# Products of the identity with itself in six waits of TensorE in the first stage of a quantised cross-attention and expert kernel

## The chip, the cores and the metric

The kernel runs on one core of one Trainium2 chip. The metric is the device time of one execution in microseconds (us). A core has TensorE (PE, matrix products; PEld is its weight load), VectorE (DVE), ScalarE (ACT), GpSimd (POOL) and SyncE (SP, which here only issues DMAs). Each engine works through its own instruction stream in order; semaphores tie the streams together. TensorE writes into eight banks of PSUM (`bank0` to `bank7`, `A[0]` to `A[7]` in the code), from which DVE and ACT read. [...]

## The reference, cut to what matters

Four batches of 256 tokens with 256 features go through two residual blocks. The first, per batch, is a gated pair of int8-style linear layers ("smooth quant"): each operand is scaled by factors of its columns' largest magnitudes, rounded row by row to -127..127, multiplied, and scaled back. The second is a mixture of eight experts with low-rank additions to shared base weights, two experts per token.

```
def _smooth_quant_linear(x, w):
    amax_x = max(abs(x), axis=0);  amax_w = max(abs(w), axis=0)
    s = sqrt(maximum(amax_x, EPS) / maximum(amax_w, EPS))
    xs = x / s;  ws = w * s
    x_scale = max(abs(xs), axis=-1) / 127;  w_scale = max(abs(ws), axis=-1) / 127
    return round(xs / x_scale) @ round(ws / w_scale).T * x_scale * w_scale.T

gate, up = split(_smooth_quant_linear(xe, guw));  a = silu(gate) * up
x = x + tanh(g_xattn) * _smooth_quant_linear(a, dw)      # per batch, on layernorm(x)
x = x + tanh(g_ffn) * experts(layernorm(x))              # g = x@base_gate + x@gate_A[e]@gate_B[e]*0.25, ...
```

## The kernel before

All streams are written out by hand, one function per engine; what an engine does next is the next line of its function, and it waits there for the semaphores named.

The first stage (to about 55 us) is the first block, batch by batch (`b` = 0 to 3, two tiles of 128 tokens each), with the batches interleaved. For TensorE one batch is this sequence:

- `w_T(b)`, `x_T1(b)`, `c_T(b)`: transposes of the weights, of the normalised tokens and of the second weight, from which DVE takes the column maxima (`w_max`, `x_max`, `c_max`; `c_max` increments `s_camax`). `c_T(b)` writes bank `4 + b`.
- `factors(b)` (line 1520): four f32 products that spread the smoothing factors (computed on POOL) over all partitions, each with the identity `ident` as moving operand. DVE's `smooth(b)` (lines 1077 to 1084) multiplies by them, takes row maxima and their inverses.
- `q1_T(b)` (line 1537): eight transposes in two halves of the values that ACT scaled (line 694), into banks `b` and `4 + b`. ACT copies them out as bf16 (line 702).
- `row_w(b)` (1520, two products), `products1(b)` (1550): the row of weight scales, and the quantised product itself. DVE (1092), ACT (709, 719) and DVE (1098, `act_up`) scale it back, apply silu and multiply.
- `a_T(b)` (1557): two transposes of the result, for DVE's `a_max` (1109, 1110). From it POOL makes the second factors (519).
- `factors2(b)` (1520), then DVE `smooth2` (1116 to 1121), ACT (724), `q2_T(b)` (1569), ACT (731), `row_c(b)` (1520), `products2(b)` (1582). DVE then adds the residual and normalises again (`x1_rows`, `x1_norm`, 1128 to 1146).
- `x2_T(b)` (1590) transposes the normalised tokens for the second block; ACT (741) and DVE (1151) split them into two parts.

From about 55 us TensorE runs 32 `unit`s, the products with the shared base weights (lines 56, 58, 60, called as `split_product`), six products of 448 columns each, with the last pieces of the first stage and the routing logits between the first of them. DVE computes the routing from the logits (lines 1224 to 1313), and POOL then gathers the sorted tokens (561). The expert tiles follow to the end.

Bank 7 (`A[7]`) holds `w_T(3)` and `c_T(3)` at first, and is written again by the second half of `q1_T(3)` and by the routing counts at line 1712. Bank 4 is written by `c_T(0)` and then by the second half of `q1_T(0)`.

Of the kernel before, what the change touches and what calls it, by code (L numbers as in the profile page):

```python
# [32 lines left out]
P = 128  # L33
# [16 lines left out]
def products_of(m):  # L50

    def split_product(outs, hi, lo, whi, wlo, first, last):

        n = len(outs)
        for i in range(n):
            m.matmul(outs[i], hi, whi[i], start=first, stop=False, skip_group_check=True)  # L56
        for i in range(n):
            m.matmul(outs[i], hi, wlo[i], start=False, stop=False, skip_group_check=True)  # L58
        for i in range(n):
            ins = m.matmul(outs[i], lo, whi[i], start=False, stop=last, skip_group_check=True)  # L60
        return ins

    return split_product


def build(nc, x, fside, ctxw, g_xattn, g_ffn, wealth, conf_W, conf_b,
          base_gate, base_up, base_down, gate_A, gate_B, up_A, up_B, down_A, down_B, xn, gun, yg, out):
    NB, S, H = x.shape
    I2 = ctxw.shape[2]
    E, _, R = gate_A.shape  # L70
    I = base_gate.shape[1]
    ER = E * R
# [17 lines left out]
    with stack:  # L90
        def sem(name):
            return stack.enter_context(nc.semaphore(name))

        def sb(name, shape, dt=F32, scope=stack):
            return scope.enter_context(nc.sbuf_tensor(name, shape, dt))

        def ps(name, shape, dt=F32, scope=stack):
            return scope.enter_context(nc.psum_tensor(name, shape, dt))
# [3 lines left out]
        ident = sb("ident", [P, P])  # L102
# [26 lines left out]
        with part1:  # L129
            def s1(name, shape, dt=F32):  # L130
                return sb(name, shape, dt, part1)
# [37 lines left out]
            count = s1("count", [P, G])  # L169
# [96 lines left out]
        with psum:  # L266
            A = [ps(f"bank{i}", [P, 512], F32, psum) for i in range(8)]
# [18 lines left out]
        s_wamax, s_xamax, s_camax, s_ratio, s_srs = sem("s_wamax"), sem("s_xamax"), sem("s_camax"), sem("s_ratio"), sem("s_srs")  # L286
# [1196 lines left out]
        def _(pe):  # L1483
            m = nc.tensor
            pe.wait_ge(s_ident, 1)
            pe.wait_ge(s_identb, 1)
            split_product = products_of(m)

            def w_T(b):
                pe.wait_ge(d_w[b], 16)  # L1490
                for c in range(HC):
                    for j in range(TB):
                        ins = m.transpose(A[4 + b][:, c * S + j * P:c * S + (j + 1) * P], q1[:, b, 2 + j, c * P:(c + 1) * P], ident[:, :])
                ins.then_inc(s_wT, 1)

            def x_T1(b):
                pe.wait_ge(s_xn, TB * (b + 1))
                if b == NB - 1:
                    pe.wait_ge(s_cWT, 1)
                for c in range(HC):  # L1500
                    for j in range(TB):
                        ins = m.transpose(A[b][:, c * S + j * P:c * S + (j + 1) * P], q1[:, b, j, c * P:(c + 1) * P], ident[:, :])
                ins.then_inc(s_xT1, 1)

            def c_T(b):
                pe.wait_ge(d_c[b], 16)
                pe.wait_ge(s_wamax, b + 1)
                for j in range(TB):
                    ins = m.transpose(A[4 + b][:, j * P:(j + 1) * P], q2[:, b, 2 + j, :], ident[:, :])
                ins.then_inc(s_cT, 1)  # L1510
# [7 lines left out]
            def along_rows(to, column, unit_rows):  # L1518

                return m.matmul(to, column.to_broadcast([P, P]), unit_rows[:, :], start=True, stop=True)  # L1520

            def factors(b):
                pe.wait_ge(s_srs, b + 1)
                for w in range(2):
                    for c in range(HC):
                        o = (w * HC + c) * P
                        ins = along_rows(A[b][:, o:o + P], s_rs[:, b, c, w:w + 1], ident)
                ins.then_inc(s_bc, 1)

            def q1_T(b):  # L1530
                pe.wait_ge(s_camax, b + 1)
                for w in range(2):
                    pe.wait_ge(s_scaled, 4 * b + 2 * w + 2)
                    for c in range(HC):
                        for j in range(TB):
                            o = (c * TB + j) * P
                            ins = m.transpose(A[b + 4 * w][:, o:o + P], q1[:, b, 2 * w + j, c * P:(c + 1) * P], ident[:, :])
                    ins.then_inc(s_q1Tp, 1)
# [7 lines left out]
            def products1(b):  # L1546
                pe.wait_ge(s_q1T, 2 * b + 2)
                for j in range(TB):
                    for c in range(HC):
                        ins = m.matmul(A[b][:, j * S:(j + 1) * S], q1T[:, b % 2, 0, c, j * P:(j + 1) * P],  # L1550
                                       q1T[:, b % 2, 1, c, :], start=(c == 0), stop=(c == HC - 1))
                ins.then_inc(s_mm1, 1)

            def a_T(b):
                pe.wait_ge(s_a, b + 1)
                for j in range(TB):
                    ins = m.transpose(A[b][:, j * P:(j + 1) * P], q2[:, b, j, :], ident[:, :])
                ins.then_inc(s_aT, 1)
# [7 lines left out]
            def q2_T(b):  # L1566
                pe.wait_ge(s_scaled2, 4 * b + 4)
                for i in range(4):
                    ins = m.transpose(A[4 + b][:, i * P:(i + 1) * P], q2[:, b, i, :], ident[:, :])
                ins.then_inc(s_q2Tp, 1)  # L1570

            def row_c(b):
                pe.wait_ge(s_q2T, b + 1)
                pe.wait_ge(s_identg, 1)
                for j in range(TB):
                    ins = along_rows(A[4 + b][:, j * P:(j + 1) * P], sc2[:, b, 2 + j:3 + j], identg)
                ins.then_inc(s_cbc, 1)

            def products2(b):
                pe.wait_ge(s_q2T, b + 1)  # L1580
                for j in range(TB):
                    ins = m.matmul(A[b][:, j * H:(j + 1) * H], q2T[:, b % 2, 0, j * P:(j + 1) * P], q2T[:, b % 2, 1, :],
                                   start=True, stop=True)
                ins.then_inc(s_mm2, 1)
# [47 lines left out]
            def base(t):  # L1632

                for u in range(4 * t, 4 * t + 4):
                    unit(u)

            w_T(0)
            x_T1(0)
            w_T(1)
# [7 lines left out]
            c_T(1)  # L1647
            c_T(2)
            c_T(3)
            q1_T(0)  # L1650
            factors(1)
            row_w(0)
            products1(0)
            factors(2)
            x_T1(3)
            q1_T(1)
            a_T(0)
            row_w(1)
            products1(1)
# [3 lines left out]
            row_w(2)  # L1663
            products1(2)
            q2_T(0)
            row_c(0)
            products2(0)
            a_T(1)
            q1_T(3)
            factors2(1)  # L1670
# [52 lines left out]
            for g in range(NG):  # L1723
                ins = m.matmul(A[6][:, 0:4 * PT], atrow[:, g, :], attrib[:, g].rearrange("p a j -> p (a j)"),
                               start=(g == 0), stop=(g == NG - 1))
# [6 lines left out]
            for g in range(NG):  # L1732
                ins = m.matmul(A[6][:, 256:256 + 3 * LATE], atrow[:, g, :], lateb[:, g].rearrange("p a i -> p (a i)"),
                               start=(g == 0), stop=(g == NG - 1))
# [186 lines left out]
            for i in range(LATE):  # L1921
                pe.wait_ge(s_ylo, i + 1)
                for b in range(NB):
                    for y in (y_hi, y_lo):
                        for t in range(TB):
                            q = (TB * b + t) * P
                            ins = m.matmul(late_bank(b)[:, t * H:(t + 1) * H], onehot[:, i, q:q + P], y[:, i, :],
                                           start=(i == 0 and t == 0 and y is y_hi), stop=(i == LATE - 1), skip_group_check=True)
# [34 lines left out]
```

## Time and profile before

| | |
|---|---|
| timed runs | 267.85, 271.71, 272.23 us (median 271.71) |
| profiled execution | 270.51 us; span from the first to the last instruction 268.3 us |
| mean granted clock of TensorE over the span | 0.959 |
| PE busy | 239.5 us (89%), 1550 matmul records |
| DVE, ACT, POOL busy | 192.0 (72%), 180.6 (67%), 138.7 us (52%) |
| chain that ended last, by engine | PE 67%, DVE 11%, DMA 7%, POOL 6% |

The span is the time between the first and the last instruction of the program on the core; the time of an execution has about 2.2 us around it. In a timeline each row stands for one or several like instructions in a row: start from the span's beginning, length from the first one's start to the last one's end, engine, source line, operation, what is written and read, and how many. A bracket gives the idle time of the engine just ahead of it and what ended the wait. Matmuls overlap: a row lasts past the start of the next, so the time that a group takes on TensorE is read from start to start.

### The profile page before, as it was taken

The numbers are of one execution on the slowest core, as the hardware profiler recorded it, in microseconds if no ns is written. First come the engines' busy times: TensorE is split into PE (matmuls) and PEld (weight loads), VectorE is DVE, ScalarE is ACT, GpSimd is POOL, SyncE is SP. The second block draws the span as 40 slices with busy tenths as digits, with TensorE's granted clock in tenths as the row PEclk, the third lists the DMA queues.
The fourth block names the chain that finished last, engine by engine and source line by source line (L and its number), as shares of the span: only waits on it lengthen the run. The fifth ranks groups of instructions, "written<-read, shape, count | busy, mean of one in ns | idle before, by whom it ended". The sixth has DMA issues, their size and how long they took to land.

```text
span 268.3 us, 5005 instructions
## 1 busy us (share of the span) xinstructions
PE 239.5 (89%) x1550; PEld 218.2 (81%) x1550; DVE 192.0 (72%) x403; ACT 180.6 (67%) x390; POOL 138.7 (52%) x160
## 2 busy tenths in 40 slices
PE   0748596899989999999998999999999999999883
PEld 0647384699979998889987999999999999998772
DVE  2799968797668962437786687777777777777664
ACT  2738989889674545858998576666666666665450
POOL 4787865684851011278573645884444555531051
PEclk9997868589999999999999999999999999999998
DMA  5963541646897557555527325555555555440644
GB/s 150 331 187 79 124 129 34 170 114 233 248 263 267 205 191 284 174 151 184 176 61 274 104 96 176 176 178 176 178 176 177 177 177 172 159 161 20 187 148 156
DMA packets 31348, 45.78 MB, mean 171 GB/s; under 512 B 14104, under 2 KB 25760, under 8 KB 31328
## 3 DMA queue, kind: packets, MB, share of 16 engines
q0 software_dynamic: 4416, 21.50, 23.9%
q1 hardware_dynamic: 20752, 14.03, 18.7%
q10 hardware_dynamic: 6160, 9.98, 10.4%
q8 instruction: 13, 0.21, 0.4%
q14 instruction: 7, 0.06, 0.1%
HBM read 33.57 MB, written 11.93 MB: 170 GB/s over the span
## 4 chain that ended last, share of the span: by engine, by line
PE 67%; DVE 11%; DMA 7%; POOL 6%; issue 4%; ACT 3%; ACTq 1%; SPq 0%; DVEq 0%; POOLq 0%
PE pY L56 6%; PE pY L58 6%; PE pY L60 6%; PE bank L56 5%; PE bank L58 5%; PE bank L60 5%; PE pT L1800 4%; PE bank L1520 3%; POOL held_B L605 3%; PE pG L1789 2%; PE pG L1790 2%; DMA xin<-normed,tok 2%; PE pU L1790 2%; PE pU L1789 2%; DMA yr<-results 2%
## 5 line engine op out<-in xcount | busy, mean ns | idle before, releaser
L56 PE MATMUL pY<-Wd_hi,hT_hi 128*128 128x320 f32 (+1 forms) x126 | 42.0, 334 | 0.1
L60 PE MATMUL pY<-Wd_hi,hT_lo 128*128 128x320 f32 (+1 forms) x126 | 39.7, 315 | 0.0
L58 PE MATMUL pY<-Wd_lo,hT_hi 128*128 128x320 f32 (+1 forms) x126 | 39.7, 315 | 0.0
L569 POOL DMA_INDIRECT bin<-base_products,tok x18 | 24.8, 1376 | 23.0 <-DVE hbuf L1370 21.6
L561 POOL DMA_INDIRECT xin<-normed,tok x19 | 18.5, 972 | 30.3 <-DVE share L1313 14.0
L575 POOL DMA_INDIRECT results<-yb,dest x17 | 16.9, 992 | 24.6 <-ACT yb L919 23.3
L752 ACT COPY brow<-bank 128x448 f32<-128x448 f32 x32 | 16.9, 531 | 14.2 <-PE bank L60 13.7
L1380 DVE TENSOR_TENSOR hT_lo<-pT,hT_hi 128x512 fp32r<-128x512 f32 (+1 forms) x38 | 23.4, 619 | 3.2 <-ACT hT_hi L896 2.3
L56 PE MATMUL bank<-Wbase_hi,x2T_hi 128*128 128x448 f32 x64 | 24.8, 387 | 0.2 <-ACT brow L752 0.2
L56 PEld LDWEIGHTS pY<-Wd_hi,hT_hi 128*128 128x128 f32 x126 | 23.7, 188 | 0.6 <-ACT Wd_lo L885 0.5
L58 PEld LDWEIGHTS pY<-Wd_lo,hT_hi 128*128 128x128 f32 x126 | 23.8, 189 | 0.0
L60 PEld LDWEIGHTS pY<-Wd_hi,hT_lo 128*128 128x128 f32 x126 | 23.7, 188 | 0.0
L58 PE MATMUL bank<-Wbase_lo,x2T_hi 128*128 128x448 f32 x64 | 23.3, 364 | 0.0
L60 PE MATMUL bank<-Wbase_hi,x2T_lo 128*128 128x448 f32 x64 | 23.2, 363 | 0.0
L1385 DVE TENSOR_TENSOR zT_lo<-pY,zT_hi 128x128 fp32r<-128x128 f32 x18 | 5.2, 291 | 24.4 <-ACT zT_hi L913 24.4
L896 ACT CAST hT_hi<-pT 128x512 fp32r<-128x512 f32 (+1 forms) x38 | 20.8, 549 | 1.4 <-PE pT L1800 1.3
L491 POOL TENSOR_TENSOR WB<-raw,WB 128x448 fp32r<-128x448 f32 x16 | 18.0, 1141 | 7.0 <-ACT WB L663 6.9
L1800 PE MATMUL pT<-ident,hbuf 128*128 128x128 f32 x133 | 20.6, 272 | 0.0
L1375 DVE TENSOR_TENSOR hbuf<-hbuf,gb 128x896 f32<-128x896 f32 x18 | 19.5, 1083 | 0.1
L1365 DVE TENSOR_TENSOR gb<-pG,bin 128x896 f32<-128x896 f32 x18 | 19.4, 1080 | 0.0
L1370 DVE TENSOR_TENSOR hbuf<-pU,bin 128x896 f32<-128x896 f32 x18 | 19.4, 1079 | 0.0
L1800 PEld LDWEIGHTS pT<-ident,hbuf 128*128 128x128 f32 x133 | 16.7, 141 | 3.1 <-DVE hbuf L1444 0.3
(331 smaller groups left out, 723.1 us busy)
## 6 DMA issues: line engine op xcount, KB each, us to landing
base_products<-brow ACTq DMA_DIRECT2D x16, 448.0 KB, 3.6
yr<-results SPq DMA_DIRECT2D x8, 256.0 KB, 5.6
raw<-in_L_ffn_gate_B_dram SPq DMA_DIRECT2D x8, 224.0 KB, 2.5
raw<-in_L_ffn_up_B_dram SPq DMA_DIRECT2D x8, 224.0 KB, 2.7
raw<-in_L_ffn_down_A_dram SPq DMA_DIRECT2D x7, 256.0 KB, 4.6
x_resid<-in_x_dram SPq DMA_DIRECT2D x4, 256.0 KB, 5.1
q<-in_fside_BxS2xS_dram ACTq DMA_DIRECT2D x4, 256.0 KB, 6.8
normed<-q ACTq DMA_DIRECT2D x4, 256.0 KB, 3.9
```

The costliest lines, as they stand in the source:

```text
L56: m.matmul(outs[i], hi, whi[i], start=first, stop=False, skip_group_check=True)
L58: m.matmul(outs[i], hi, wlo[i], start=False, stop=False, skip_group_check=True)
L60: ins = m.matmul(outs[i], lo, whi[i], start=False, stop=last, skip_group_check=True)
L491: g.tensor_tensor(lo, src, hi, ALU.subtract).then_inc(s_wlo, 1)
L561: g.indirect_dma_start(out=xin[:, :], out_offset=None, in_=xn, in_offset=bass.IndirectOffsetOnAxis(ap=tok[:, j:j + 1], axis=0)).then_inc(d ...
L569: g.indirect_dma_start(out=bin_[:, (j + 1) % 2].rearrange("p a i -> p (a i)"), out_offset=None, in_=gun, in_offset=bass.IndirectOffsetOnAx ...
L896: a.copy(hT_hi[:, h_chunks(i), :].rearrange("p c q -> p (c q)"), h_bank(i)).then_inc(s_hhi, 1)
L1365: v.tensor_tensor(halves(gb[:, :]), pG[:, :, 0:IH], halves(bin_[:, 1 - slot, 0, :]), ALU.add).then_inc(s_gadd, 1)
L1370: v.tensor_tensor(halves(hbuf[:, :]), pU[:, :, 0:IH], halves(bin_[:, 1 - slot, 1, :]), ALU.add).then_inc(s_uadd, 1)
L1375: v.tensor_tensor(hbuf[:, :], hbuf[:, :], gb[:, :], ALU.mult).then_inc(s_h, 1)
L1380: v.tensor_tensor(hT_lo[:, h_chunks(i), :].rearrange("p c q -> p (c q)"), h_bank(i), hT_hi[:, h_chunks(i), :].rearrange("p c q -> p (c q)" ...
L1800: ins = m.transpose(pT[:, i, (c % 4) * P:(c % 4 + 1) * P], hbuf[:, c * P:(c + 1) * P], ident[:, :])
```

## The change

In the function of TensorE a helper `spare_products(bank, count)` issues `count` f32 products of the 128x128 identity with itself into the first 128 columns of a bank. Nothing reads the result. It is called six times: 30 products ahead of `q1_T(0)` into bank 4, and into bank 7 seven ahead of `x_T1(3)`, five ahead of `q1_T(1)`, nine ahead of `a_T(0)`, five ahead of `row_c(0)` and eight ahead of `a_T(1)`, 64 in all. Two waits on `s_camax` stand ahead of the first and the second call, so that DVE has read what the bank held. Nothing else changes on any engine.

```
@@ -1486,6 +1486,11 @@
+            def spare_products(bank, count):
+
+                for _ in range(count):
+                    m.matmul(bank[:, 0:P], ident[:, :], ident[:, :], start=True, stop=True, skip_group_check=True)
+
             def w_T(b):
@@ -1647,13 +1652,19 @@
             c_T(1)
             c_T(2)
             c_T(3)
+            pe.wait_ge(s_camax, 1)
+            spare_products(A[4], 30)
             q1_T(0)
             factors(1)
             row_w(0)
             products1(0)
             factors(2)
+            pe.wait_ge(s_camax, NB)
+            spare_products(A[7], 7)
             x_T1(3)
+            spare_products(A[7], 5)
             q1_T(1)
+            spare_products(A[7], 9)
             a_T(0)
             row_w(1)
             products1(1)
@@ -1663,8 +1674,10 @@
             row_w(2)
             products1(2)
             q2_T(0)
+            spare_products(A[7], 5)
             row_c(0)
             products2(0)
+            spare_products(A[7], 8)
             a_T(1)
             q1_T(3)
             factors2(1)
```

The order of TensorE's stream before, from `c_T(3)` (line 1509, bank 7) to `products1(0)`:

```order
L1509 MATMUL bank7<-ident,q2 128x128 x2
L1537 MATMUL bank0<-ident,q1 128x128 x4
L1537 MATMUL bank4<-ident,q1 128x128 x4
L1520 MATMUL bank1<-ident,s_rs 128x128 x4
L1520 MATMUL bank4<-ident,sc1 128x128 x2
L1550 MATMUL bank0<-q1T 128x256 x4
```

The same place after the change, where the lines of the file stand five further down:

```order
L1514 MATMUL bank7<-ident,q2 128x128 x2
L1492 MATMUL bank4<-ident 128x128 x30
L1542 MATMUL bank0<-ident,q1 128x128 x4
L1542 MATMUL bank4<-ident,q1 128x128 x4
L1525 MATMUL bank1<-ident,s_rs 128x128 x4
L1525 MATMUL bank4<-ident,sc1 128x128 x2
L1555 MATMUL bank0<-q1T 128x256 x4
```

The thirty products stand between the last transposes of the second weights and `q1_T(0)`; a row names each operand once, so `bank4<-ident` has the identity as both. TensorE's stream before, from `q2_T(0)` (line 1569) to the first half of `q1_T(3)`:

```order
L1569 MATMUL bank4<-ident,q2 128x128 x4
L1520 MATMUL bank4<-identg,sc2 128x128 x2
L1582 MATMUL bank0<-q2T 128x256 x2
L1557 MATMUL bank1<-ident,q2 128x128 x2
L1537 MATMUL bank3<-ident,q1 128x128 x4
```

And after the change:

```order
L1574 MATMUL bank4<-ident,q2 128x128 x4
L1492 MATMUL bank7<-ident 128x128 x5
L1525 MATMUL bank4<-identg,sc2 128x128 x2
L1587 MATMUL bank0<-q2T 128x256 x2
L1492 MATMUL bank7<-ident 128x128 x8
L1562 MATMUL bank1<-ident,q2 128x128 x2
L1542 MATMUL bank3<-ident,q1 128x128 x4
```

Five products stand ahead of `row_c(0)` and eight between `products2(0)` and `a_T(1)` (line 1562).

## Rows read from the trace of the kernel before

**Rows 1.** Table by stretches: length, busy us of each engine, granted clock, DMA, GB/s.

```profile
21.10:24.52 3.42, 3.42 (x16) 3.21 (x16) 3.21 (x12) 3.42 (x8) 2.73 (x3) 0.50 0.13 29
24.52:31.34 6.82, 4.00 (x30) 3.07 (x28) 6.45 (x15) 5.36 (x12) 5.54 (x9) 1.00 0.52 117
31.34:38.17 6.83, 6.21 (x28) 5.62 (x29) 4.69 (x14) 5.99 (x12) 6.08 (x6) 0.50 0.43 121
38.17:45.00 6.83, 4.45 (x33) 3.13 (x31) 5.52 (x13) 6.17 (x16) 1.85 (x3) 1.00 0.28 84
45.00:55.24 10.24, 8.65 (x35) 7.02 (x36) 8.53 (x23) 9.15 (x19) 7.09 (x8) 0.50 0.42 115
55.24:117.00 61.76, 61.00 (x397) 55.16 (x397) 39.70 (x124) 40.98 (x86) 24.10 (x28) 1.00 0.68 216
...
44.50:50.00 5.50, 3.81 (x15) 2.77 (x15) 5.29 (x15) 4.65 (x11) 5.29 (x7) 0.55 0.31 83
```

**Rows 2.** Timeline of TensorE: start, length, line, instruction, [idle before, what ended it].

```profile
14.50 1.06 PE L1520 MATMUL bank<-ident,s_rs 128*128 128x128 f32 x8
15.39 0.60 PE L1502 MATMUL bank<-ident,q 128*128 128x128 f32 x4
15.83 0.82 PE L1509 MATMUL bank<-ident,q 128*128 128x128 f32 x6
21.10 2.00 PE L1537 MATMUL bank<-ident,q 128*128 128x128 f32 x8 [4.46 <-ACT q L694]
22.91 1.83 PE L1520 MATMUL bank<-ident,s_rs 128*128 128x128 f32 x8
...
27.69 0.66 PE L1502 MATMUL bank<-ident,q 128*128 128x128 f32 x4 [1.11 <-ACT q L677]
29.15 0.63 PE L1537 MATMUL bank<-ident,q 128*128 128x128 f32 x4 [0.81 <-ACT q L694]
...
31.96 0.69 PE L1557 MATMUL bank<-ident,q 128*128 128x128 f32 x2 [1.26 <-DVE q L1098]
32.54 1.23 PE L1520 MATMUL bank<-ident,sc 128*128 128x128 f32 x4
...
39.49 0.66 PE L1569 MATMUL bank<-ident,q 128*128 128x128 f32 x4
40.93 0.71 PE L1520 MATMUL bank<-identg,sc 128*128 128x128 f32 x4 [0.78 <-ACT q2T L731]
...
42.95 0.44 PE L1557 MATMUL bank<-ident,q 128*128 128x128 f32 x2 [1.09 <-DVE q L1098]
...
49.57 1.11 PE L1590 MATMUL bank<-ident,q 128*128 128x128 f32 x4 [0.92 <-DVE q L1146]
```

**Rows 3.** Timeline of DVE in the first stage.

```profile
24.87 1.28 DVE L1077 TENSOR_TENSOR q<-q,bank 128x512 f32<-128x512 f32 x2 [0.20 <-PE bank L1520]
...
34.81 0.88 DVE L1092 SCALAR_TENSOR_TENSOR hq<-bank,sc,rowb 128x256 f32<-128x256 f32 x2 [1.02 <-ACT rowb L709]
...
37.23 0.18 DVE L1121 RECIPROCAL inv<-sc 128x4 f32<-128x4 f32 x1
38.74 1.28 DVE L1077 TENSOR_TENSOR q<-q,bank 128x512 f32<-128x512 f32 x2 [1.33 <-PE bank L1520]
...
42.48 0.41 DVE L1098 TENSOR_TENSOR q<-bank,hq 128x256 f32<-128x256 f32 x1
43.42 0.42 DVE L1109 TENSOR_REDUCE amx<-bank 128x1 f32<-128x256 f32 x1 [0.53 <-PE bank L1557]
```

**Rows 4.** Timeline of ACT in the first stage.

```profile
23.24 1.25 ACT L702 ACTIVATE q1T<-bank,rounder 128x512 bf16<-128x512 f32 x2
```

**Rows 5.** Timeline of POOL: the first gather of rows.

```profile
95.80 1.23 POOL L561 DMA_INDIRECT xin<-normed,tok  x1 [14.03 <-DVE share L1313]
```

**Rows 6.** Timeline of TensorE: the first transposes of gathered rows.

```profile
100.68 0.42 PE L1750 MATMUL pX<-ident,xin 128*128 128x128 f32 x2
```

**Rows 7.** DMA issues: queue, operation, count, median us from issue to landing.

```profile
xin<-normed,tok POOLq DMA_INDIRECT x19, 4.3
```

More of the change, by code:

```diff
@@ L1487, in _, with spare_products @@
             split_product = products_of(m)
+            def spare_products(bank, count):
+                for _ in range(count):
+                    m.matmul(bank[:, 0:P], ident[:, :], ident[:, :], start=True, stop=True, skip_group_check=True)
             def w_T(b):
@@ L1649, in _ @@
             c_T(3)
+            pe.wait_ge(s_camax, 1)
+            spare_products(A[4], 30)
             q1_T(0)
@@ L1654, in _ @@
             factors(2)
+            pe.wait_ge(s_camax, NB)
+            spare_products(A[7], 7)
             x_T1(3)
+            spare_products(A[7], 5)
             q1_T(1)
+            spare_products(A[7], 9)
             a_T(0)
@@ L1665, in _ @@
             q2_T(0)
+            spare_products(A[7], 5)
             row_c(0)
             products2(0)
+            spare_products(A[7], 8)
             a_T(1)
```

## The prediction

> **What bounds the kernel now.** I read the table by stretches first, cut where the granted clock changes [rows 1]. TensorE falls to half clock three times in the first stage: at 21.10, after it had stood idle for 4.46 us [rows 2]; at 31.34, after a stretch in which it worked 4.00 of 6.82 us; and at 45.00, after 4.45 of 6.83 us. It is back at full clock at 24.52, 38.17 and 55.24. [...] From 55.24 to 117.00 it works 61.00 of 61.76 us at full clock. So an earlier or later start of the base products at 55 moves everything behind it, as long as nothing else becomes the limit.
>
> The first stage itself is not TensorE's. The timeline of its instructions [rows 2] has a wait in brackets before each of the six places: 4.46, 1.11, 0.81, 1.26, 0.78 and 1.09 us, all ended by ACT or DVE. The DVE timeline [rows 3] shows the counterpart: DVE waits 0.20, 1.33 and 0.53 us for TensorE, and 1.02 us for ACT. From 44.5 to 50.0 DVE works 5.29 of 5.50 us [rows 1], and TensorE waits 0.92 us for it before 49.57 [rows 2].
>
> **The price of one filler.** No instruction of before multiplies the identity by itself. The nearest row is L1520: f32, 128x128, with the identity as the moving operand. Four of them are issued by `factors(0)`, and the trace records eight matmuls: from 14.50 to the next row at 15.39, 0.89 us, so 0.2225 us for one at full clock [rows 2]. A transpose, also f32 128x128, has one record: four from 15.39 to 15.83, 0.11 us each. A filler is not marked as a transpose, so I take 0.2225; 0.11 is the lower bound. At half clock the eight records of `factors(1)` span 1.83 us instead of 1.06 [rows 2]; less the 0.17 by which the row at 14.50 outlasts the next start, 0.41 us for one, the upper bound.
>
> [...]
>
> **The change, run by run.** The 64 fillers cost 64 x 0.2225 = 14.2 us, and the six waits hold 9.5 us. Each run is therefore longer than its wait. The two new semaphore waits cost nothing: the maximum over the first context block was taken before `c_T(3)` could start, and the last one lies on DVE before the row at 24.87, where TensorE needs it only after 26.
>
> First run: the six transposes at 15.83 end their issue at 16.49. 30 x 0.2225 = 6.68, so `q1_T(0)` starts at 23.17 instead of 21.10, 2.07 late. It and `factors(1)` now run at full clock: 8 x 0.11 = 0.88, then 1.06 as at 14.50, done at 25.11. Before they were done at 22.91 + 1.83 = 24.74 [rows 2]. Behind them waits DVE (row at 24.87, only 0.20 idle before it): about 0.3 late. On ACT the copies at 23.24 [rows 4] now wait for the first half of `q1_T(0)`, 23.17 + 0.44 + 0.17 = 23.78; they take 1.25, so `row_w(0)` starts at about 25.07 and with `row_w(0)` 0.45, `products1(0)` 0.44 and `factors(2)` 0.89 the next run of fillers can start at 26.85.
>
> Second to fourth run: 7 x 0.2225 = 1.56, so `x_T1(3)` starts at 28.41 instead of 27.69. Nobody waits for it: the waits of DVE there [rows 3] are for other work. It takes 0.44, then five fillers 1.11: `q1_T(1)` at 29.96 instead of 29.15, and with 0.88 it is issued by 30.84. Nine fillers, 2.00: `a_T(0)` at 32.84 instead of 31.96, 0.9 late. At full clock it takes 0.22 instead of 0.58, so DVE's maximum over it is 0.6 late. That is covered by the 1.02 us that DVE waits for ACT before 34.81; without that cover the 0.6 would go on.
>
> What comes back: in 31.34 to 38.17 TensorE was at half clock for 6.21 us of work [rows 1]. At full clock it has the factors of block 3 well before DVE wants them, so the 1.33 us that DVE waited before 38.74 are gone. DVE is then bound by itself: its instruction at 37.23 ends at 37.41, plus the 0.3 above, 37.7 instead of 38.74 [rows 3]. Gain on DVE: 1.0 us, so its product at 42.48 is done at 41.9 instead of 42.9.
>
> Fifth and sixth run: `q2_T(0)` follows ACT and DVE and stays where it was, from 39.49; 0.44, then five fillers 1.11, 41.04 against 40.93 for `row_c(0)`; 0.45 and 0.22 for `row_c(0)` and `products2(0)`, 41.71. Now `a_T(1)` could run at 41.95, with DVE's gain. But eight fillers stand before it: 41.71 + 1.78 = 43.49, against 42.95. It is **0.5 late instead of 1.0 early**, and DVE's maximum at 43.42, which waited for it already, is 0.5 late too. This run decides: it takes the whole gain and half a microsecond more.
>
> Behind it no run of fillers stands until the base products. DVE, with next to no idle time between 44.5 and 50 [rows 1], brings `x2_T(0)` at 49.57 0.5 late. TensorE again waits for it, as in 45.00 to 55.24, where it worked 8.65 of 10.24 us at half clock; so I expect the clock to fall between 45 and 50 and to be back at about 55. The base products start 0.5 later, but less of their work lies ahead of the rise: 0.5 us at half clock become 0.25 at full. The end of the stage is then 0.25 to 0.5 late, I take 0.4. With TensorE busy from there to 117.00, and no stage behind with a new instruction, it goes through to the end.
>
> The sum: 270.5 (the profiled execution; its span is 268.3, 2.2 lie around it) + 0.4 = **270.9**. That execution stands 1.2 below the median of the timed runs, 271.71.
>
> **The rivals.** *The clock comes back later.* TensorE's work before 55.24 now begins 0.5 late, and the stretch had 1.6 us without work already [rows 1]. If the rise slips, it is at least by the shortest stretch at half clock in the trace, 3.4 us. Half of that, 1.7, is lost on base products: 270.5 + 0.4 + 1.7 = 272.6. For it: the work that preceded the rise begins later, the rise does not wait for it. Against: the waits behind 49.57 are the same ones. It decides if the clock is still at half at 56.
>
> *A filler has one record, as a transpose has*: 0.11 us. The runs are then 3.3, 0.8, 0.6, 1.0, 0.6 and 0.9 us, each within its wait, and nothing is late. DVE keeps its 1.0 us; `a_T(1)` runs at 40.93 + 0.67 + 0.88 = 42.5, 0.45 early: 270.1. Against: the L1520 rows.
>
> *Full clock through 45 to 55 as well*, since TensorE enters it with less idle behind it. It is then limited by the first gather of rows, issued at 95.80 behind DVE's routing: at the median of 4.3 us to landing its data are there at 100.1, and TensorE takes them at 100.68 [rows 5 to 7]. With DVE 0.5 late they are there at 100.6, so no more than 0.1 is gained: 270.4. Against: none of the waits behind 43 is filled.
>
> *The fillers don't hold the clock*, so that it falls as before and the thirty run mostly at half clock: 30 x 0.41 = 12.3 us, `q1_T(0)` at 28.8, 7.7 late, little of it covered since DVE stands behind it: about 278. It decides if the clock falls before about 20. Against: full clock at 14.50 to 16.5 was reached and held by transposes and L1520 alone.
>
> **How the numbers follow.** The forecast 0.57, the late rise 0.2, the short filler 0.08, full clock throughout 0.05, fillers that don't hold it 0.05, and 0.05 for a gain that I don't see. A measurement of this kernel can tell about 2%, 5.4 us, from no change; its three runs lie from 267.85 to 272.23. Only the fillers at half clock are slower by more, only the unseen gain faster: slower 0.05, faster 0.05, within 2% 0.90. The range: the forecast less what the lowest run lies below the profiled one (270.9 - 2.7 = 268.2), up to the late rise with a little for the upper runs, 273.0.
>
> **What would show it.** In the profile after: 128 records of fillers, 0.11 us apart; `q1_T(0)` at about 23.2; full clock from 14 to past 45; DVE's smoothing of block 3 near 37.7 with no wait for TensorE before it; `a_T(1)` near 43.5, straight behind fillers; a fall of the clock between 45 and 50 and a rise near 55 (near 58 in the first rival). The prediction is wrong if the fillers have 64 records or lie further apart, if DVE's gain at 37.7 is missing, if `a_T(1)` comes before 42.95, or if the clock falls in the first run.

## The result, and the profile of the changed kernel

The changed kernel takes 272.62 us (median of 4 runs, 271.51 to 275.00) against 271.58 us for the kernel before on the same chip (4 runs); ratio 1.0121, 95% interval 1.0066 to 1.0177. Timed once more with 12 runs against 35 it took 272.84 us against 271.37: ratio 1.0079, 1.0042 to 1.0116. The ratios leave out runs classed as slow (8 of those 35, none of the 12), and stand above the ratios of the medians given, 1.0038 and 1.0054. So the changed kernel is slower, by 0.4 to 1.2%. The time lies in the predicted range, and within 2% as forecast, but the sum had said +0.4 us for the change. The loss is 1.0 and 1.5 us by the medians, 1.6 us between the two profiled executions, and 2.1 to 3.3 us by the ratios.

| | before | after |
|---|---|---|
| profiled execution | 270.51 us | 272.15 us |
| span | 268.3 us | 269.9 us |
| mean granted clock over the span | 0.959 | 0.979 |
| PE busy | 239.5 us (89%), 1550 records | 248.2 us (92%), 1678 records |
| at half clock (granted 0.50) ahead of 117 us | 21.10:24.52, 31.34:38.17, 45.00:55.24 | 50.51:57.34, 77.82:81.23 |

The mean clock is higher and the time is longer. The table by stretches of the kernel after (length; busy us of PE, PEld, DVE, ACT, POOL; granted clock; DMA share; GB/s) answers [rows 1]:

```profile
22.90:50.51 27.61, 22.41 (x191) 20.61 (x189) 23.23 (x60) 23.72 (x51) 19.99 (x23) 1.00 0.37 96
46.50:50.51 4.01, 1.18 (x11) 0.74 (x8) 3.87 (x12) 2.06 (x6) 3.84 (x5) 1.00 0.40 114
50.51:57.34 6.83, 6.28 (x24) 5.11 (x24) 5.13 (x14) 5.45 (x11) 3.94 (x6) 0.50 0.51 134
57.34:77.82 20.48, 19.88 (x136) 18.47 (x135) 13.33 (x33) 16.45 (x36) 13.30 (x16) 1.00 0.74 225
77.82:81.23 3.41, 3.41 (x11) 3.05 (x10) 3.02 (x11) 1.66 (x4) 1.17 (x2) 0.50 1.15 263
```

The first two stretches at half clock of before are gone. The third has moved: it no longer lies on the waits of the first stage but from 50.51 to 57.34, over the first base products. A new one, 77.82 to 81.23, lies wholly on base products. TensorE's timeline shows why the third moved; it answers [rows 2] (lines stand five further down, L1492 is the identity product):

```profile
15.22 1.12 PE L1514 MATMUL bank<-ident,q 128*128 128x128 f32 x6
16.18 6.86 PE L1492 MATMUL bank<-ident 128*128 128x128 f32 x60
22.88 1.04 PE L1542 MATMUL bank<-ident,q 128*128 128x128 f32 x8
...
28.27 0.60 PE L1507 MATMUL bank<-ident,q 128*128 128x128 f32 x4
28.71 1.28 PE L1492 MATMUL bank<-ident 128*128 128x128 f32 x10
29.82 1.04 PE L1542 MATMUL bank<-ident,q 128*128 128x128 f32 x8
30.70 2.17 PE L1492 MATMUL bank<-ident 128*128 128x128 f32 x18
32.71 0.38 PE L1562 MATMUL bank<-ident,q 128*128 128x128 f32 x2
...
40.84 0.61 PE L1525 MATMUL bank<-identg,sc 128*128 128x128 f32 x4
41.28 0.38 PE L1587 MATMUL bank<-q2T 128*128 128x256 bf16 x2
41.50 1.95 PE L1492 MATMUL bank<-ident 128*128 128x128 f32 x16
43.29 0.38 PE L1562 MATMUL bank<-ident,q 128*128 128x128 f32 x2
...
46.27 0.60 PE L1555 MATMUL bank<-q1T 128*128 128x256 bf16 x4
49.69 0.66 PE L1595 MATMUL bank<-ident,q 128*128 128x128 f32 x4 [2.83 <-DVE q L1146]
...
54.94 0.72 PE L56 MATMUL bank<-Wbase_hi,x2T_hi 128*128 128x448 f32 x1
```

No wait in brackets stands before the filled places any more. But `products1(3)` now runs at 46.27 at full clock, where it ran at 47.59 at half clock before, and so the wait ahead of `x2_T(0)` has grown from 0.92 us [rows 2] to 2.83 us. `x2_T(0)` itself is only 0.12 late, the first base product 0.08 (54.94 instead of 54.86).

DVE's timeline answers [rows 3]:

```profile
24.94 1.28 DVE L1077 TENSOR_TENSOR q<-q,bank 128x512 f32<-128x512 f32 x2 [0.26 <-PE bank L1525]
...
33.13 0.42 DVE L1109 TENSOR_REDUCE amx<-bank 128x1 f32<-128x256 f32 x1 [0.56 <-PE bank L1562]
...
34.88 0.88 DVE L1092 SCALAR_TENSOR_TENSOR hq<-bank,sc,rowb 128x256 f32<-128x256 f32 x2 [0.66 <-ACT rowb L709]
...
37.42 1.28 DVE L1077 TENSOR_TENSOR q<-q,bank 128x512 f32<-128x512 f32 x2
...
41.16 0.41 DVE L1098 TENSOR_TENSOR q<-bank,hq 128x256 f32<-128x256 f32 x1
43.71 0.42 DVE L1109 TENSOR_REDUCE amx<-bank 128x1 f32<-128x256 f32 x1 [2.13 <-PE bank L1562]
```

DVE gets 1.32 us ahead (38.74 to 37.42), has its product at 41.16, and then stands 2.13 us for `a_T(1)`, which waits behind the eight fillers at 41.50. It is 0.29 late afterwards (43.42 to 43.71).

### The profile page after: what moved, and what is told of

Read it like the earlier page. It is cut to its first block, busy times and chain, and to the rows that moved or that the text cites. A ratio compares the mean times of both kernels' runs of the same rounds, so it can differ in the third digit from the quotient of the medians.

```text
span 269.9 us, 5261 instructions
## 1 busy us (share of the span) xinstructions
PE 248.2 (92%) x1678; PEld 228.7 (85%) x1678; DVE 192.1 (71%) x403; ACT 180.9 (67%) x390; POOL 138.6 (51%) x160
## 4 chain that ended last, share of the span: by engine, by line
PE 64%; DMA 11%; ACT 7%; POOL 6%; DVE 6%; issue 4%; ACTq 1%; SPq 0%; DVEq 0%; POOLq 0%
PE pY L56 6%; PE pY L58 5%; PE pY L60 5%; PE bank L56 5%; PE bank L58 5%; PE bank L60 5%; DMA xin<-normed,tok 4%; PE pT L1813 4%; PE bank L1492 4%; POOL held_B L605 3%; PE pG L1802 2%; PE pG L1803 2%; DMA q<-in_ctx_dram 2%; PE pU L1803 2%; PE pU L1802 2%
## 5 line engine op out<-in xcount | busy, mean ns | idle before, releaser
L56 PE MATMUL bank<-Wbase_hi,x2T_hi 128*128 128x448 f32 x64 | 25.6, 400 | 0.0
L58 PE MATMUL bank<-Wbase_lo,x2T_hi 128*128 128x448 f32 x64 | 24.4, 381 | 0.0
L60 PE MATMUL bank<-Wbase_hi,x2T_lo 128*128 128x448 f32 x64 | 24.3, 379 | 0.0
```

## The experiments

Three theories. **Theory 1**: the loss is lateness, from runs of fillers longer than their waits, above all the eight ahead of `a_T(1)`. **Theory 2**: the loss is where the clock now stands behind 50, a late rise at 57.34 and the fall at 77.82. **Theory 3**: each filler costs its time wherever it stands. The two new semaphore waits are no theory of their own: they stand in all kernels below but one, and several of those beat the kernel before. Each kernel was timed in 12 runs beside 35 runs of before on the same chip, in three batches: the two kernels with the sixth run alone or longer, the one without it and the fitted one with the clock held (before 271.09 us); the fitted one, the one with three products more, the transposes and the changed kernel again (271.37); the last four (270.97). Ratios are to before of the same batch. The edits are against the changed kernel.

The starts (us) that the readings use, from the profiles:

| | `a_T(1)` | `x2_T(0)` | first base product | last logits | counts (L1712 of before) | half clock from 45 to 117 |
|---|---|---|---|---|---|---|
| before | 42.95 | 49.57 | 54.86 | 74.75 | 82.77 | 45.0:55.2 |
| after | 43.29 | 49.69 | 54.94 | 75.78 | 84.86 | 50.5:57.3, 77.8:81.2 |
| after, second profile | 42.98 | 49.38 | 54.62 | 75.51 | 84.59 | 50.3:57.2, 77.6:81.1 |
| without the sixth run | 41.30 | 48.25 | 53.49 | 74.67 | 83.75 | 49.3:56.2, 76.6:80.0 |
| sixth run alone | 44.50 | 50.95 | 55.68 | 76.08 | 85.16 | 51.4:54.8, 78.7:82.1 |
| fitted runs | 41.45 | 48.40 | 53.69 | 74.07 | 82.09 | 47.6:54.4 |
| fitted, clock held | 41.46 | 48.41 | 53.14 | 73.56 | 81.56 | none |
| after, clock held ahead of `x2_T(0)` | 43.01 | 49.41 | 54.14 | 74.55 | 83.63 | 77.2:80.6 |

**Without the sixth run.**

```
             row_c(0)
             products2(0)
-            spare_products(A[7], 8)
             a_T(1)
```

> The changed kernel without the eight products ahead of `a_T(1)`; the other 56 stay. Theory 1 (the sixth run takes the stage's gain away): `a_T(1)` starts at about 41.9 instead of 43.29, `x2_T(0)` at about 48.4 instead of 49.69, and the time is 1.0 to 1.4 us under the changed kernel, ratio to the kernel before about 1.007 or less. Theory 2 (what costs is where TensorE's clock stands in the base products: back at 57.34 instead of 55.24, and down again from 77.82 to 81.23): `x2_T(0)` may come earlier, but the time stays near that of the changed kernel, ratio about 1.012, as long as the clock is at half somewhere between 52 and 82.

Measured: 269.87 us, ratio 0.9963 (0.9924 to 1.0001). TensorE's timeline at the place:

```profile
41.30 0.44 PE L1562 MATMUL bank<-ident,q 128*128 128x128 f32 x2
...
48.25 0.66 PE L1595 MATMUL bank<-ident,q 128*128 128x128 f32 x4 [1.85 <-DVE q L1146]
```

`a_T(1)` comes 1.99 earlier than in the kernel after, `x2_T(0)` 1.44; against the second profile of that kernel, whose first run of fillers starts at nearly the same time, it is 1.68 and 1.13. The ratio is 0.0116 to 0.0158 lower. Eight products of 1.78 us are worth the whole loss or more. Theory 1 holds for this run, though the times gain more than the trace shows at `x2_T(0)`. Theory 2 is not touched: half clock still lies at 49.3 to 56.2 and at 76.6 to 80.0.

**The sixth run alone.** The other five runs and both new waits are taken out, `spare_products(A[7], 8)` ahead of `a_T(1)` stays.

> Only the eight products ahead of `a_T(1)`; the other five runs are taken out. Theory 1: TensorE reaches this place as late as in the kernel before, at about 41.8 after `products2(0)`, so `a_T(1)` starts at about 43.6 instead of 42.95 and the time is 0.5 to 0.8 us over the kernel before, ratio 1.002 to 1.003. Theory 2: the clock falls in the first stage as in the kernel before, the share at half clock in the base products is as there, ratio 1.00. Theory 3 (each filler costs its time, wherever it stands): eight of 64, an eighth of the loss, ratio 1.0015.

Measured: 272.68 us, ratio 1.0046 (1.0006 to 1.0086).

```profile
41.13 3.58 PE L1492 MATMUL bank<-ident 128*128 128x128 f32 x16
44.50 0.43 PE L1562 MATMUL bank<-ident,q 128*128 128x128 f32 x2
...
50.95 0.72 PE L1595 MATMUL bank<-ident,q 128*128 128x128 f32 x4 [2.83 <-DVE q L1146]
```

At half clock, granted from 41.2 to 44.6 there, the eight take 3.37 us, 0.42 each, and fit the wait of 1.09 [rows 2] still less. `x2_T(0)` is 1.38 late. Alone they cost 1.25 us by the ratio, with an interval from 0.2 to 2.3. That is not the price of lateness alone, since half clock behind 50 lies elsewhere than in the kernel before, and the interval leaves Theory 1 and Theory 3 standing.

**The sixth run twice as long.**

```
-            spare_products(A[7], 8)
+            spare_products(A[7], 16)
```

> The changed kernel with 16 instead of eight products ahead of `a_T(1)`. Theory 1: 8 x 0.2233 = 1.79 us more in front of `a_T(1)`, which starts at about 45.1; DVE waits for it, and as nothing behind it has slack, the whole 1.8 us goes to the end: 1.8 us over the changed kernel, ratio about 1.019. Theory 2: the time moves by less than 1 us unless the stretches at half clock behind 50 change.

Measured: 273.62 us, ratio 1.0075 (1.0037 to 1.0113); in its profile `a_T(1)` at 45.41, `x2_T(0)` at 51.82, the first base product at 56.54, 1.60 later than in the kernel after for 1.78 us of products (`x2_T(0)` is 2.13 later, 0.33 of it because the first run of fillers starts later). Yet the ratio is not above that of the changed kernel (1.0079). Its stretch at half clock is shorter, 51.9 to 55.3, and is over before the base products begin. In its 12 runs the mean granted clock has a median of 0.986, against 0.977 in those of the changed kernel. So what the products cost by lateness, the clock seems to have given back in part, and Theory 2 would then have a part. It is a sign and no proof: the 1.78 us are 0.0066 of the time, the two intervals are 0.004 wide to either side, and by the medians this kernel stands 2.5 us over before and the changed one 1.5.

**Runs that fit their waits.** 21, 5, 4, 6 and 4 products instead of 30, 7, 5, 9 and 5, none ahead of `a_T(1)`:

```
-            spare_products(A[4], 30)
+            spare_products(A[4], 21)
...
-            spare_products(A[7], 7)
+            spare_products(A[7], 5)
...
-            spare_products(A[7], 8)
```

> The five runs cut to what fits into their waits (21, 5, 4, 6, 4), none ahead of `a_T(1)`, and no new runs behind it. Theory 1: as the kernel with the two new runs up to 43, `a_T(1)` at about 41.5 and `x2_T(0)` at 48.4; the clock then falls between 45 and 50, is at half through the start of the base products and costs 1 us or more there: ratio 0.995, against 0.989 with the new runs. Theory 2 (the clock behind 50 is all that counts): the stage's earlier end brings nothing without it, ratio 1.00. If the new runs did nothing: 0.989.

Measured: 269.32 us, ratio 0.9930 (0.9886 to 0.9975). The stage is at full clock up to 47.55 (granted 1.00, then 0.50 to 54.4), and `q1_T(0)` at 21.22, where it was without any filler (21.10).

**The same, and the clock held up to the base products.** Six products more ahead of `row_w(3)` and seven ahead of `x2_T(0)`, into bank 2, behind a wait for its last reader:

```
+            pe.wait_ge(s_deq1, 3)
+            spare_products(A[2], 6)
             row_w(3)
             products1(3)
+            spare_products(A[2], 7)
             x2_T(0)
```

> The first five runs cut to what fits into their waits (21, 5, 4, 6, 4 instead of 30, 7, 5, 9, 5), none ahead of `a_T(1)`, and two new runs: six ahead of `row_w(3)` and seven ahead of `x2_T(0)`, into bank 2, behind a wait for DVE's reading of that bank. Theory 1: nothing that DVE or ACT waits for is late, `a_T(1)` at about 41.7, `x2_T(0)` at 48.2, so 1.2 us or more under the kernel before, ratio 0.99 to 0.996. Theory 2: if in addition the clock stays at full through 50 to 58, the base products start at 53 and another 1.5 us is gained, ratio about 0.99; if the clock falls all the same, ratio about 1.00. Theory 3 (each filler costs): 53 of 64, ratio 1.010.

Measured: 268.86 us, ratio 0.9891 (0.9846 to 0.9936). The table by stretches:

```profile
13.26:52.54 39.28, 33.31 (x261) 28.93 (x261) 34.02 (x86) 32.06 (x68) 27.87 (x30) 1.00 0.47 129
53.00:76.00 23.00, 21.97 (x147) 20.25 (x146) 16.49 (x41) 18.13 (x40) 16.76 (x19) 1.00 0.70 217
76.00:100.00 24.00, 23.84 (x172) 21.35 (x172) 19.81 (x77) 12.82 (x26) 4.14 (x4) 1.00 0.68 224
```

Full clock throughout, 53 fillers in the stage, and faster than both kernels. Theory 3 falls: by it 53 x 0.2225 = 11.8 us would have been lost, or a ratio of 1.010 if each filler bore its share of the measured loss. Against the fitted runs without the hold the first base product is 0.55 earlier; the two ratios, 0.9930 and 0.9891, are not told apart.

**Fitted, held, and three products more ahead of the last logits.**

```
             unit(8)
+            pe.wait_ge(s_resid, 3)
+            spare_products(A[2], 3)
             logits(3)
```

> The kernel with fitting runs and the two new ones, and three more products ahead of the last logits, into bank 2, behind a wait for ACT's reading of that bank; they fill the 0.60 us that TensorE waits for DVE there. Theory: half clock near 77 to 82, as in the traces of the changed kernel and of three experiments, comes after the logits, whose products have eight columns; with the fillers it is rarer, and the time is 0 to 1 us under the kernel without them, ratio 0.985 to 0.989. If those falls have another cause, 0.07 us later and ratio 0.989; if the three fillers outlast their wait by 0.1 us and nothing else, 0.990.

Measured: 268.72 us, ratio 0.9911 (0.9878 to 0.9944): not told apart from the one without the three. Its 12 runs lie within 1.75 us, those without the three within 5.05.

**Transposes in place of products.** The 64 at the same places and counts, `m.transpose` of the identity instead of `m.matmul`.

> The same six runs with the same counts, but transposes of the identity (one record each, 0.11 us) instead of products. Each run then fits into its wait (3.3, 0.8, 0.55, 1.0, 0.55, 0.9 us). If lateness decides, `a_T(1)` starts at about 42.5 and the time is 0.4 to 1 us under the kernel before, ratio 0.996 to 0.999. If transposes don't hold the clock at full, it falls before 21 or at 31, as in the kernel before, and the ratio is 1.00.

Measured: 270.11 us, ratio 0.9952 (0.9917 to 0.9988).

```profile
16.80 3.44 PE L1492 MATMUL bank<-ident 128*128 128x128 f32 x30
21.15 0.63 PE L1542 MATMUL bank<-ident,q 128*128 128x128 f32 x4 [0.91 <-ACT q L694]
```

and its table by stretches:

```profile
16.70:48.98 32.28, 23.57 (x185) 19.90 (x184) 28.59 (x75) 26.67 (x57) 23.29 (x27) 1.00 0.43 112
```

One record and 0.11 us each: the second rival's filler, made on purpose. The thirty leave 0.91 us of their wait, and the same 64 instructions now gain 0.5% where they lost 0.8%. So the price of one filler against its wait counts, as Theory 1 says. It is not lateness alone here either: behind the stage half clock lies at 49.0 to 52.4, over before the first base product at 53.28, and at 76.3 to 79.7. The transposes keep the granted clock at 1.00, here from 16.70 to 48.98, as the products do (from 12.96 to 50.51 in the kernel after).

**The changed kernel again**, unchanged, for a second profile.

> The changed kernel once more, on the chip and beside the runs of the three below. Theory 1 (the sixth run and the lateness of the others): between the kernel without the sixth run and the one with sixteen there, ratio 1.000 to 1.004. Theory 2 (the clock behind 50 costs about as much again): 1.008 to 1.012, as in its first measurement. In the trace: clock at half from about 50 to 57 and perhaps again near 78.

Measured: 1.0079, as given above.

```profile
49.38 0.66 PE L1595 MATMUL bank<-ident,q 128*128 128x128 f32 x4 [2.83 <-DVE q L1146]
54.62 0.72 PE L56 MATMUL bank<-Wbase_hi,x2T_hi 128*128 128x448 f32 x1
```

Half clock lies from 50.3 to 57.2 and from 77.6 to 81.1: the two stretches behind 50 came again. In this execution nothing is late ahead of the base products: `x2_T(0)` is 0.19 and the first base product 0.24 earlier than in the kernel before. Even so the last logits are 0.76 and the counts 1.82 later. Here the two stretches at half clock make the whole delay at the counts, without any lateness.

The last four kernels separate the two parts; the first three of them leave the fillers of the change as they are.

**The change, and the clock held ahead of `x2_T(0)`.**

```
+            pe.wait_ge(s_deq1, 3)
+            spare_products(A[2], 11)
             x2_T(0)
```

> The changed kernel (64 products) with a seventh run of 11 identity products ahead of x2_T(0), into bank 2, behind the wait on s_deq1: 11 x 0.2225 = 2.45 us, inside the 2.83 us that TensorE waits there in the profile after. Nothing ahead of it changes, so x2_T(0) stays at about 49.4 to 49.7. Theory 2 (the second cause is where the clock stands behind 50): no stretch at half clock from 50 to 57, first base product near 54.2, and of the 2.4 us of base products at half clock 1.2 come back: about 1.5 us less than the changed kernel, 271.2, ratio to before 1.002. A fall at 74 to 78 can still be there. Theory 1 (only the 8 products ahead of a_T(1) and what is late behind them): same as the changed kernel, 272.7, ratio 1.008. Theory 3 (each product costs its time wherever it stands): 2.4 us more, 275.1, ratio 1.015.

Measured: 271.21 us, ratio 1.0014 (0.9984 to 1.0044).

```profile
46.43 2.62 PE L1492 MATMUL bank<-ident 128*128 128x128 f32 x22
49.41 0.66 PE L1595 MATMUL bank<-ident,q 128*128 128x128 f32 x4 [0.37 <-DVE q L1146]
...
54.14 0.45 PE L56 MATMUL bank<-Wbase_hi,x2T_hi 128*128 128x448 f32 x1
```

As Theory 2 had it: nothing ahead of `x2_T(0)` has changed, no half clock at 50 to 57, the first base product 0.8 earlier than in the kernel after, the logits 1.23. Of both, 0.28 was there at `x2_T(0)` already; against the second profile of the changed kernel it is 0.48 and 0.96. Eleven more products, 2.45 us, make the kernel faster by 0.0065 to 0.0107 of its time, 1.8 to 2.9 us. By the medians it is 0.24 us over before, where the changed kernel is 1.0 and 1.5 over, so the gain is 0.8 to 1.2 us, about what the profiles show. Theory 1's 1.008 lies outside the interval. The mean granted clock of the 12 runs has a median of 0.994, against 0.977.

Not all that the clock gives arrives: with the hold TensorE waits 0.43 us for DVE ahead of `x2_T(1)`, at 61.26, where neither the kernel before nor the one after has a wait.

**The change, and three products ahead of the last logits** (the edit shown above).

> The changed kernel with three identity products more, ahead of logits(3), into bank 2, behind the wait on s_resid: 0.67 us in the idle time of 0.60 us that stands before the last logits at 75.78 in the profile after. Theory 2: where the clock fell behind these logits (77.82 to 81.23), it no longer does; 9 base products at 0.373 instead of 0.2025 us are 1.5 us at most, less the 0.1 that the three products outlast the wait. Half clock from 50.5 to 57.3 stays. About 1.0 less than the changed kernel, 271.7, ratio 1.004. If that fall is a matter of where a stretch begins and not of these waits, it comes elsewhere and the ratio stays 1.008. Theory 1: the same as the changed kernel, 1.008. Theory 3: 0.7 us more, 1.010.

Measured: 272.09 us, ratio 1.0037 (1.0002 to 1.0073). Its table by stretches:

```profile
50.97:57.80 6.83, 5.82 (x20) 5.01 (x21) 5.13 (x13) 5.23 (x11) 4.38 (x5) 0.50 0.44 129
57.80:100.00 42.20, 42.03 (x287) 38.65 (x287) 32.38 (x108) 27.85 (x60) 17.22 (x19) 1.00 0.71 220
```

The fall at 77.8 is missing, the late rise is there, and the counts begin at 83.89 instead of 84.86: 1.0, of which 0.18 was there at the first base product (54.76). By the ratios it is 0.4% less than the changed kernel, in line with Theory 2; the two intervals overlap.

**Both.**

> Both together: 11 products ahead of x2_T(0) and three ahead of logits(3), 78 in all. Theory 2: full clock from 13 to past 100; x2_T(0) at 49.4 to 49.7, first base product near 54.2 against 53.15 in the kernel whose runs fit their waits and whose clock is held in the same two places (0.991). What is left against that one is lateness alone, 1.0 us: ratio 0.995, 270.0 us. Theory 1: all of the loss is lateness, so no gain on the changed kernel, 1.008. Theory 3: 3 us more than the changed kernel, 1.019.

Measured: 271.50 us, ratio 1.0028 (1.0000 to 1.0056). Theory 2 had said 0.995, so this missed, and it is no faster than the kernel without the three products (1.0014). The clock is as expected, granted 1.00 from 15.37 to past 100. TensorE's timeline shows what was not, in this execution:

```profile
14.01 1.06 PE L1507 MATMUL bank<-ident,q 128*128 128x128 f32 x4
14.86 1.30 PE L1525 MATMUL bank<-ident,s_rs 128*128 128x128 f32 x8
16.00 0.60 PE L1507 MATMUL bank<-ident,q 128*128 128x128 f32 x4
16.43 0.82 PE L1514 MATMUL bank<-ident,q 128*128 128x128 f32 x6
17.09 6.86 PE L1492 MATMUL bank<-ident 128*128 128x128 f32 x60
23.79 1.04 PE L1542 MATMUL bank<-ident,q 128*128 128x128 f32 x8
```

The four transposes at 14.01 still take 0.21 each (14.01 to 14.86), half clock; those at 16.00 take 0.11. The clock rose for the first time at 15.37, in the kernel after at 12.96. The thirty begin 0.91 later, and since no wait is left ahead of `q1_T(0)`, it is 0.91 late too (23.79 against 22.88), and `a_T(1)`, at 44.21, 0.92. In the seven profiles with thirty products these begin between 15.84 and 17.09, and `q1_T(0)` starts 6.70 behind, from 22.54 to 23.79. In the fitted kernels they begin between 15.98 and 16.53, and `q1_T(0)` always starts between 21.13 and 21.22. There is a second reason why so little was gained. The fall at 77 is not in every run of the kernel without the three products: six of its 12 have a mean granted clock of 0.996 or more, and a stretch of 3.41 us at half clock, as in its profile, would alone bring it to 0.9937. In those six there was next to nothing for the three products to give back.

With the clock alike at both places, the kernel with the fillers of the change stands at 1.0028 and the fitted one, timed in another batch, at 0.9911. The difference, 0.0117 or 3.2 us, is the price of fillers that outlast their waits, as far as two batches can be compared. Their profiles give 2.2 at the first base product (55.34 to 53.15) and 2.5 in the span (269.0 to 266.5); 0.92 of it is the later start that the fitted kernel would have absorbed. The two kernels without the three products, whose first runs of fillers start at nearly the same time (15.89 and 15.98), show 1.0 at the first base product (54.14 to 53.14).

**Fitted, held, and `x2_T(0)` made late.**

```
-            spare_products(A[2], 7)
+            spare_products(A[2], 14)
             x2_T(0)
```

> The kernel whose runs fit their waits, with the clock held ahead of row_w(3), x2_T(0) and logits(3) (0.991), and 14 instead of 7 products ahead of x2_T(0): 7 x 0.2225 = 1.56 us more in a wait that had 0.28 us left. It measures what lateness costs where the clock stays at full. x2_T(0) at 49.65 instead of 48.43. If the whole of it goes on to the base products and through to the end, as the prediction said of the stage behind 55: first base product 54.35, 269.9 us, ratio 0.9955. If the waits of 0.63 and 0.90 us that TensorE still has between x2_T(0) and the base products take it up: first base product near 53.2, ratio 0.991. Theory 2 with nothing but the clock: 0.991, since no product is taken from a place that holds it.

Measured: 269.22 us, ratio 0.9931 (0.9896 to 0.9965), against 0.9911 with seven.

```profile
46.23 3.29 PE L1492 MATMUL bank<-ident 128*128 128x128 f32 x28
49.36 0.60 PE L1595 MATMUL bank<-ident,q 128*128 128x128 f32 x4
...
51.34 0.44 PE L1562 MATMUL bank<-ident,q 128*128 128x128 f32 x2 [0.72 <-DVE q L1098]
...
52.97 0.45 PE L56 MATMUL bank<-Wbase_hi,x2T_hi 128*128 128x448 f32 x1
```

`x2_T(0)` stands 0.93 later than with seven, and the first base product is not late (52.97 against 53.15; from `a_T(1)` it is 11.67 in both): the waits that TensorE had behind it take it up. By this trace lateness at `x2_T(0)` itself costs nothing at the base products. The times do not decide it: both forecasts, 0.991 and 0.9955, lie in the interval. Lateness at `a_T(1)` costs, because DVE waits there (2.13 us ahead of 43.71 in the kernel after), and what DVE does after it is late; the kernel without the sixth run shows it.

## Why the prediction was wrong, step by step

**Right.** A filler costs 0.2225 us: sixty records from 16.18 to 22.88, 6.70 us for thirty, 0.2233 each. The clock stays at full through the first five runs (granted 1.00 up to 50.51). `x_T1(3)` at 28.27 (28.41 forecast), `q1_T(1)` at 29.82 (29.96), `a_T(0)` at 32.71 (32.84). DVE's maximum is 0.44 late there, and 0.66 of its wait for ACT is still left to cover it. DVE smooths block 3 at 37.42 with no wait (37.7). `a_T(1)` stands at 43.29 (43.49), straight behind the eight. "This run decides" was right: without it the ratio is 0.9963.

**Somewhat off.** `q1_T(0)` came at 22.88, not 23.17, because the clock first rose at 12.96 instead of 14.28 (four transposes take 0.44 us from 13.45 there, 0.65 from 13.85 in the kernel before) and the thirty could start at 16.18. The working took this start as fixed; over seven profiles it runs from 15.84 to 17.09. `x2_T(0)` was 0.12 late, not 0.5. (The working has two slips without weight: 23.78 + 1.25 is 25.03, not 25.07, and the base products at half clock in the kernel before are 0.38 us, not 0.5.)

The third rival's limit did not hold either. It let full clock up to 55 gain no more than 0.1, because of the first gather. In the fitted, held kernel the gather is issued 1.20 earlier (94.60 instead of 95.80), as the last logits come 1.19 earlier: the gather moves with them.

As a time, 270.9 lies below the median of before, since the sum starts from the profiled execution; what it said of the change is +0.4.

**The step that failed** is the term behind 43: "the clock to fall between 45 and 50 and to be back at about 55", and its price of 0.25 to 0.5. The clock fell at 50.51 and rose at 57.34. The argument was that the waits behind 49.57 are the same. They nearly are (0.31 us before; 0.17 and 0.38 after); but the wait ahead of 49.57 is not. TensorE, at full clock, is done with `products1(3)` earlier while DVE is not, so 0.92 us of wait became 2.83, and from 46.50 to 50.51 TensorE worked 1.18 of 4.01 us. Then came half clock. The base products at half clock were 0.38 us (54.86 to 55.24) and are 2.40 us (54.94 to 57.34); half of the difference is 1.01. The trace shows 0.95 more lag at the last logits (from 0.08 to 1.03). That is the first rival, "the clock comes back later", with its sign ("still at half at 56") seen; its 1.7 was too much, since it was taken from the shortest stretch at half clock and not from where the base products begin. The experiment that fills this wait (1.0014 instead of 1.0079 to 1.0121, no half clock from 50 to 57) shows the cause.

**A step that was missing.** "It goes through to the end" held no second fall. From 77.82 to 81.23 nine base products start 0.373 instead of 0.2025 us apart, and the lag grows by 1.06, to 2.09 at the counts. The nine starts make 1.53; the kernel before loses some of that time to a wait that the changed one does not have:

```profile
80.17 0.47 PE L56 MATMUL bank<-Wbase_hi,x2T_hi 128*128 128x448 f32 x1 [0.16 <-ACT brow L752]
```

Of the lag 0.5 comes back by the end of the span (+1.6); but from the counts to the end the 14 profiles take 184.1 to 186.6 us, so half a microsecond there says little. So the first rival's 272.6 agrees with the measured 272.62 by luck: it was a figure for the profiled execution, which took 272.15, its stretch cost 1.0 and not 1.7, and the rest came from a fall that it did not have.

What this fall costs is read from the profiles alone. Three products ahead of the last logits lower the ratio in one of three pairs (1.0079 to 1.0037, 1.0014 to 1.0028, 0.9891 to 0.9911), and in none beyond the intervals.

Why that fall comes is not settled. Between the last `x2_T` and the base products behind the last logits both kernels do the same work. The stretches, first of before:

```profile
72.10:76.30 4.20, 3.60 (x26) 3.16 (x26) 0.82 (x3) 2.62 (x6) 2.54 (x4) 1.00 1.07 268
```

and of after:

```profile
73.10:77.30 4.20, 3.60 (x26) 3.15 (x26) 0.84 (x2) 2.68 (x6) 2.55 (x3) 1.00 1.09 272
```

The first is followed by full clock, the second by half clock 0.5 us later. The four profiles with three products ahead of the last logits do not have the fall, but neither have the fitted ones without them. So no cause is claimed.

**The balance.** The clock's gain, with fillers that fit and with the hold, is 0.9 to 1.1%, 2.4 to 3.0 us. The change spends 3.2 us on fillers that outlast their waits, and gives up another 1.8 to 2.9 us at half clock behind 50. That makes between 2.0 and 3.7 us net; measured are 2.1 to 3.3. All these figures are differences of the same ratios, so that they add up proves nothing; the medians and the profiles put the single parts lower, at about 1 us for the half clock at 50 to 57 and 1.0 to 2.2 us at the first base product for the fillers.

## What to carry to other kernels

Fill a wait of TensorE by the price of the very instruction, taken from a row of the same type and shape, and leave room for a later start: a run that outlasts its wait delays its consumer (`q1_T(0)` 1.78 us in the first profile of the change) and passes a shift of its start on (0.91 of 0.91 us in the profile with both additions). A full clock made TensorE wait longer at the next place that is bound by another engine (2.83 us instead of 0.92), so the filling had to reach the last wait ahead of the stage that TensorE bounds: without that the half clock moved on, from the waits of the stage (45.00 to 55.24) onto the base products (50.51 to 57.34). And a higher mean clock was no gain by itself (0.979 against 0.959, at 272.15 against 270.51 us): ask which instructions lie in the half-clock stretches.

## What the runs showed that was not expected

The first rise of the clock moves from execution to execution: 11.78 to 15.37 us in the profiles here; four transposes take 0.43 us from 12.90 in the profile of the earliest, 0.85 from 14.01 in that of the latest. Without the thirty the wait ahead of `q1_T(0)` absorbs that (4.46 us and a start at 21.10 in the kernel before, 4.63 and 21.05 with the sixth run alone); with thirty fillers it reaches the end of the stage (`q1_T(0)` from 22.54 to 23.79). With the waits fitted and held at three places the 12 runs spread over 1.75 us, the 35 of before over 5.33 in the same batch (268.62 to 273.95); the like kernel with 14 products ahead of `x2_T(0)` spreads over 3.19, though, so the narrow spread is not shown to come from the hold. And transposes of the identity, at 0.11 us each, hold the clock in these waits at 1.00 (from 16.70 to 48.98), as products of 0.2233 us do. Five versions lie below the kernel before with their whole interval: fitted, the three fitted and held, and the transposes. The lowest are fitted and held, 0.9891 (0.9846 to 0.9936), and with the last logits filled as well, 0.9911 (0.9878 to 0.9944).
